# Local transformer kernel: score and weighing matmuls issued in two halves, with a turn of probabilities and a value projection between them

## The chip, the cores and the metric

The kernel runs on one core of one Trainium2 chip. The time is device microseconds of one execution; a kernel is timed several times and the median stands for it. In the rows PE is TensorE (matmuls), PEld its weight loads, DVE is VectorE, ACT ScalarE, POOL GpSimd and SP SyncE.

## The reference

The whole reference has three parts: a time-mixing layer, six layers of a local transformer, and a second block of full attention and a mixture of experts. The change lies in the local transformer, 2048 tokens of width 128 in 2 sequences of 1024:

```python
for i in range(DEPTH):                      # 6 layers
    x = attn_layer(shift_tokens(x), Wqkv[i], q_scale[i], k_scale[i], Wo[i]) + x
    x = ffn_layer(shift_tokens(x), ln_g[i], ln_b[i], W1[i], b1[i], W2[i], b2[i]) + x
...
def attn_layer(x, Wqkv, qs, ksc, Wo):       # 16 heads of 64, windows of 32 tokens
    q, k, v = jnp.split(x @ Wqkv, 3, -1)    # then split into heads
    q, k = l2norm(q) * qs, l2norm(k) * ksc
    # rotary tables on q and k
    out = local_attention(q, k, v)
    return out @ Wo
...
sim = jnp.einsum('bhwie,bhwje->bhwij', bq, bk2) * QK_SCALE   # 32 queries x 64 keys, per window
sim = jnp.where(mask, -jnp.finfo(sim.dtype).max, sim)
attn = jax.nn.softmax(sim, -1)
out = jnp.einsum('bhwij,bhwje->bhwie', attn, bv2)
```

## The kernel before

`time_mixing_and_local` runs the 6 layers as one pipeline over 96 blocks of 128 tokens (`ALL`, 16 blocks in each layer; consecutive blocks belong to the two sequences in turn). A step `i` of the loop over `STEPS` does a different stage for each of several blocks: it turns queries and keys of block i, projects queries and keys of block i+2 and values of block i+1, computes the scores of block i, turns the probabilities of block i-1 and weighs its values, turns the attention of block i-2 and projects it out. The feed-forward works on two blocks together: `variance`, `up` (and `center`) and `down` come in every other step, `up` when i is odd and `down` and `center` when i is even. Each engine has its own program with the same loop, and the order of its work is written out by hand there; the engines meet in semaphores. An engine takes its instructions in order, and so a wait holds all that stands behind it.

A block has 16 heads in 8 pairs (`PAIRS`), and 4 windows (`WPB`). Its scores are 8 x 4 x 2 products of a 64x32 tile of queries with 64 keys; each takes two weight loads and two matmul instructions, so `scores` (L648) is 128 small matmuls and `weigh_v` (L677) another 128. Before the scores, `scores` lays the mask into the two banks with two matmuls (L638, or L641 for a sequence's first blocks). `turn_prob` (L659) turns four pairs of heads at a time with four full-size transposes, and `project_v` (L602 to L604) is three matmuls of 512 columns in a reduced-precision format, high and low parts. `turn_att` is L687, `down` L730, `up` L721 and L722, `center` L707, `variance` L712, `project_out` L699.

The waits that stand ahead of the parts:

- `scores(g)` waits for the turned queries and keys, and for `shifted`, that is until VectorE has read the scores of block g-1.
- `turn_prob(g, 0)` waits for the exponentials of block g.
- `weigh_v(g)` waits for ScalarE's two copies of turned probabilities (`prob_out`, L1018), for the values' DMAs, for `av_out` of the block before, and for VectorE's first shift of block g+1 (`shifted`, L1300), since the scores and the weighed values of neighbouring blocks share three PSUM banks:

```python
SV = (0, 1, 2)
def score_bank(g, par):
    return SV[(4 * g + par) % 3]
def value_bank(g, par):
    return SV[(4 * (g + 1) + 2 + par) % 3]
```

On VectorE `shift_scores(i, 0)` is L1298 (maximum) and L1300 (subtraction), then comes a part of the feed-forward (`norm` L1335 or `finish` L1349), `shift_scores(i, 1)`, `sum_squares(i + 2)` L1271, and `norm_att` L1319. On ScalarE the copies come in the order `empty_prob` (L1018, twice), `empty_v(i + 1, 0)` (L997), `square_qk` (L978), `empty_v(i + 1, 1)`, `exponent(i)` (L1029), and at the end of the step `invert_norms(i + 2)` (L987 to L991).

Of the kernel before, what the change touches and what calls it, by code (L numbers as in the profile page):

```python
# [23 lines left out]
HD = 64  # L24
PAIRS = HEADS // 2
WIN = 32
BLK = 128
WPB = BLK // WIN
# [46 lines left out]
def time_mixing_and_local(nc, A, sb, sem, bank, ident, mean_w, eps, x_main, h_in, h_mid, mod, gate_a):  # L75
# [7 lines left out]
    with ExitStack() as ctx:  # L83
        def buf(name, shape, dt=F32):
            return sb(f"lt_{name}", shape, dt, ctx=ctx)
# [27 lines left out]
        q_t = buf("q_t", [P, 2, PAIRS, BLK])  # L113
        k_t = buf("k_t", [P, 2, PAIRS, WIN + BLK])
        v_tok = buf("v_tok", [P, 2, 2, PAIRS * HD])
        v = buf("v", [P, 2, WPB, PAIRS, HD])
# [4 lines left out]
        prob_t = buf("prob_t", [P, 2, PAIRS, BLK])  # L121
# [19 lines left out]
        S = type("S", (), sems)  # L141
# [26 lines left out]
        def last_flat(t, u):  # L168
            return t[:, 0:CH if u < B + 1 else PAIR]
# [56 lines left out]
        def live(g):  # L226
            return 0 <= g < ALL
# [15 lines left out]
        def has_look(g):  # L243
            return g % SLOTS >= 2
# [49 lines left out]
        def turn_bank(*use):  # L294
            return TURN[uses[use] % len(TURN)]
# [25 lines left out]
# [6 lines that stand above are left out]
        def looks(g):  # L327
            return 32 * ((SLOTS - 2) * (g // SLOTS) + g % SLOTS - 1)
# [4 lines left out]
        with nc.Block(no_gpsimd_drain=True) as blk:  # L333
# [261 lines left out]
            def _(pe):  # L595
# [24 lines left out]
                                          qr[:, g % 2, (4 * j + n) * P:(4 * j + n + 1) * P], ident[:, :])  # L620
                    mm.then_inc(S.turned, 1)

                def scores(g):
                    pe.wait_ge(S.turn_out, 4 * (g + 1))
                    if g == 0:
                        pe.wait_ge(S.cleared, 5)
                        pe.wait_ge(S.cast, 4)
                        pe.wait_ge(T.b_scaled, NCH)

                    if g >= 1:  # L630
                        pe.wait_ge(S.shifted, 2 * g)
                    if g >= 2:
                        pe.wait_ge(S.av_out, 2 * (g - 2) + 1)

                    for par in range(2):
                        f = slice(64 * par, 64 * par + 64)
                        if has_look(g):
                            pe.matmul(bank[:, score_bank(g, par), :], half_b[f, :, :].rearrange("p a k -> p (a k)"), mask[f, :],  # L638
                                      start=True, stop=False, skip_group_check=True)
                        else:  # L640
                            pe.matmul(bank[:, score_bank(g, par), :].rearrange("p (a k) -> p a k", a=PAIRS), ident_b[:, :],  # L641
                                      mask_first[:, :].unsqueeze(1).to_broadcast([P, PAIRS, HD]), start=True, stop=False,
                                      skip_group_check=True)
                    for hp in range(PAIRS):
                        for w in range(WPB):
                            for par in range(2):
                                f = slice(64 * par, 64 * par + 64)
                                mm = pe.matmul(bank[WIN * w:WIN * w + WIN, score_bank(g, par), hp * HD:(hp + 1) * HD],  # L648
                                               q_t[f, g % 2, hp, WIN * w:WIN * w + WIN],
                                               k_t[f, g % 2, hp, WIN * w:WIN * w + 2 * WIN],  # L650
                                               start=False, stop=True, skip_group_check=True)
                    mm.then_inc(S.scores, 1)

                def turn_prob(g, n):
                    if n == 0:
                        pe.wait_ge(S.probs, 2 * (g + 1))
                    wait_free(pe, "prob", g, n)
                    for i in range(4):
                        mm = pe.transpose(bank[:, turn_bank("prob", g, n), i * P:(i + 1) * P],  # L659
                                          prob[:, g % 2, 4 * n + i, :, :].rearrange("p a k -> p (a k)"), ident[:, :])  # L660
                    mm.then_inc(S.prob_turned, 1)

                def weigh_v(g):
                    pe.wait_ge(S.prob_out, 2 * (g + 1))
                    pe.wait_ge(s_v[g % 2], 8 * 16 * (g // 2 + 1))
                    if has_look(g):
                        pe.wait_ge(S.look, looks(g))

                    if g >= 1:
                        pe.wait_ge(S.av_out, 2 * g)  # L670
                    if live(g + 1):
                        pe.wait_ge(S.shifted, 2 * (g + 1) + 1)
                    for hp in range(PAIRS):
                        for w in range(WPB):
                            for par in range(2):
                                f = slice(64 * par, 64 * par + 64)
                                mm = pe.matmul(bank[WIN * w:WIN * w + WIN, value_bank(g, par), hp * HD:(hp + 1) * HD],  # L677
                                               prob_t[f, g % 2, hp, WIN * w:WIN * w + WIN],
                                               v[f, g % 2, w, hp, :], start=True, stop=True)
                    mm.then_inc(S.av, 1)  # L680

                def turn_att(g, n):
                    if n == 0:
# [169 lines left out]
                def last_var(u):  # L853
                    pe.wait_ge(S.last_squared, u + 1)
                    if u >= 1:
                        pe.wait_ge(S.last_scaled, u)
                    pe.matmul(last_flat(bank[:, var_bank(u), :], u), mean_w[:, :], last_flat(last_stat[:, u % 2, :], u),
                              start=True, stop=True).then_inc(S.last_var, 1)
# [36 lines left out]
                for i in STEPS:  # L895
                    if i == -1:
                        group_mean(3)
                        project_output(2)
                        second_mean(2)
                        group_var(3)  # L900
                        second_var(2)
                    if i == 0:
                        project_output(3)
                        second_mean(3)
                    for j in range(4):
                        if live(i):
                            turn_qk(i, j)
                        if live(i + 2):
                            project_qk(i + 2, j)
                        if i == 0 and j == 1:  # L910
                            second_var(3)
                    if even(i, 5) is not None:
                        variance(even(i, 5))
                    if live(i - 2):
                        turn_att(i - 2, 0)
                        turn_att(i - 2, 1)
                    if i == ALL + 1:
                        project_out(ALL - 1)
                        last_mean(0)
                    if live(i):  # L920
                        scores(i)
                    if live(i - 1):
                        turn_prob(i - 1, 0)
                        turn_prob(i - 1, 1)
                    if live(i + 1):
                        project_v(i + 1, 0)
                    if i == ALL + 2:
                        center(CHUNKS - 1)
                    if even(i, 6) is not None:
                        down(even(i, 6))  # L930
                    if i == ALL + 2:
                        last_var(1)
                    if i == ALL + 3:
                        last_mean(2)
                    if i == ALL + 4:
                        last_mean(3)
                        last_var(3)
                    if i == ALL + 5:
                        last_mean(4)
                        last_var(4)  # L940
                    if live(i + 1):
                        project_v(i + 1, 1)
                    if live(i - 1):
                        weigh_v(i - 1)
                    if even(i, 4) is not None and i != ALL + 2:
                        center(even(i, 4))
                    if even(i, 5) is not None:
                        for j in range(FB):
                            up(even(i, 5), j)
                    if i == ALL + 1:  # L950
                        last_var(0)
                        last_mean(1)
                    if i == ALL + 3:
                        last_var(2)
                    if live(i - 2) and i - 2 < ALL - 1:
                        project_out(i - 2)
# [1686 lines left out]
```

## Time and profile before

| | |
|---|---|
| median of 3 runs | 2628.64 us (2627.93 to 2630.3) |
| the profiled execution | 2627.98 us |
| its span, first to last instruction | 2626.1 us |
| mean granted TensorE clock | 0.980 |
| PE busy | 2444.7 us, 93% |
| DVE, ACT, POOL busy | 83%, 77%, 59% |

The local transformer takes the span from about 90 us to about 1640 us. The durations of matmuls are modelled and overlap, so the distances from start to start are what to read; a row of the timeline merges instructions of one line that follow each other, with their count, and in brackets the idle time before the first and what ended it.

### The profile page before, as it was taken

What the parts mean: (1) busy time and instruction counts of PE and PEld (TensorE: products, weight loads), DVE (VectorE), ACT (ScalarE), POOL (GpSimd) and SP (SyncE); (2) the same over time, 40 slices, a digit from 0 to 9 for tenths busy, and PEclk for the clock granted to TensorE, in tenths of its full rate; (3) what the DMA queues carried; (4) which work ended last, traced back from release to release, by engine and by line L of the source; (5) the groups of instructions that cost most, each with busy time, mean ns of one, the idle gap of its engine ahead of it and who ended that gap; (6) DMA issues with size and microseconds to landing.
All of it is one profiled execution on the core that took longest, in us unless ns stands there. A gap on an engine that the chain in (4) does not pass through costs nothing. (4 is left out here: it accounts for less than half of the span.)

```text
span 2626.1 us, 118521 instructions
## 1 busy us (share of the span) xinstructions
PE 2444.7 (93%) x52349; PEld 1964.5 (75%) x52349; DVE 2174.8 (83%) x2455; ACT 2025.0 (77%) x4031; POOL 1536.7 (59%) x1075
## 2 busy tenths in 40 slices
PE   6799999999999999999999999689999999997999
PEld 2478888888787888788888887467777767775787
DVE  5788888888788888888898887388888988885888
ACT  4688888888888888888888887566667666764676
POOL 3788888888788888888897885122323222322111
PEclk8899999999999999999999999899999999999999
DMA  3243434443343344334333333122222222221221
GB/s 99 53 94 92 106 77 94 96 108 83 83 96 97 81 98 100 97 84 95 96 96 78 85 82 76 36 54 52 60 59 61 56 56 59 57 53 34 82 73 41
DMA packets 275793, 202.00 MB, mean 77 GB/s; under 512 B 117569, under 2 KB 215881, under 8 KB 274249
## 3 DMA queue, kind: packets, MB, share of 16 engines
q1 hardware_dynamic: 275280, 194.42, 30.8%
q8 instruction: 414, 6.78, 1.0%
q14 instruction: 99, 0.80, 0.1%
HBM read 36.96 MB, written 1.11 MB: 14 GB/s over the span
## 5 line engine op out<-in xcount | busy, mean ns | idle before, releaser
L509 POOL TENSOR_TENSOR lt_t_sin<-lt_qk,lt_tab 128x512 f32<-128x512 f32 x384 | 684.2, 1802 | 229.2 <-DVE lt_qk L1278 226.7
L514 POOL TENSOR_TENSOR lt_qr<-lt_qr,lt_t_sin 128x1024 f32<-128x1024 f32 x192 | 456.5, 2377 | 28.7 <-POOL lt_t_sin L509 1.8
L2047 DVE TENSOR_REDUCE fa_neg_max<-bank 128x1 f32<-128x1024 f32 x256 | 301.6, 1220 | 94.4 <-PE bank L1855 93.6
L1879 PE MATMUL bank<-fa_prob_t,fa_v 32*64 32x128 f32 x16384 | 279.6, 275 | 29.7 <-issue 25.1
L1969 ACT ACTIVATE fa_prob<-bank,fa_neg_max 128x1024 f32<-128x1024 f32 x128 | 142.7, 1114 | 210.5 <-DVE fa_neg_max L2047 164.3
L2057 DVE STREAM_TRANSPOSE fa_prob_t<-fa_prob 128x1024 f32<-128x1024 f32 x256 | 302.1, 1219 | 0.0
L1879 PEld LDWEIGHTS bank<-fa_prob_t,fa_v 32*64 32x64 f32 x16384 | 241.9, 131 | 77.1 <-issue 55.7
L602 PE MATMUL bank<-lt_w_high,lt_x_high 128*128 128x512 f32 x576 | 280.0, 486 | 0.8 <-ACT lt_v_tok L997 0.4
L1278 DVE TENSOR_TENSOR lt_qk<-lt_qk,lt_rn 128x2048 f32<-128x2048 f32 x96 | 254.5, 2651 | 24.3 <-ACT lt_rn L991 23.0
L619 PE MATMUL bank<-ident,lt_qr 128*128 128x128 f32 x1536 | 233.8, 276 | 13.6 <-POOL lt_qr L514 7.5
L970 ACT COPY lt_qk<-bank 128x512 f32<-128x512 f32 x384 | 229.7, 599 | 16.5 <-POOL lt_t_sin L509 3.8
L1271 DVE TENSOR_REDUCE lt_ssq<-lt_qr 128x32 f32<-128x2048 f32 x96 | 219.0, 2281 | 25.3 <-ACT lt_qr L978 25.3
L619 PEld LDWEIGHTS bank<-ident,lt_qr 128*128 128x128 f32 x1536 | 186.8, 142 | 65.3 <-issue 16.9
L1285 DVE TENSOR_TENSOR lt_qr<-lt_qk,lt_tab 128x2048 f32<-128x2048 f32 x96 | 231.5, 2412 | 3.3
L603 PE MATMUL bank<-lt_w_low,lt_x_high 128*128 128x512 f32 x576 | 228.5, 397 | 0.5 <-issue 0.5
L604 PE MATMUL bank<-lt_w_high,lt_x_low 128*128 128x512 f32 x576 | 228.6, 397 | 0.3 <-issue 0.3
L978 ACT ACTIVATE lt_qr<-lt_qk 128x1024 f32<-128x1024 f32 x192 | 205.5, 1071 | 0.0
L699 PEld LDWEIGHTS bank<-lt_prob_t,lt_w_o 128*128 128x128 f32 x1536 | 187.9, 193 | 8.1 <-issue 1.5
L699 PE MATMUL bank<-lt_prob_t,lt_w_o 128*128 128x128 f32 x1536 | 189.1, 277 | 1.1 <-ACT lt_prob_t L1023 0.8
L1787 POOL TENSOR_TENSOR fa_att_t<-fa_att,fa_inv_all 128x512 f32<-128x512 f32 x32 | 40.7, 1271 | 237.8 <-ACT fa_att L1993 237.8
L677 PEld LDWEIGHTS bank<-lt_v,lt_prob_t 64*32 64x32 f32 x12288 | 129.0, 105 | 67.3 <-issue 65.9
L677 PE MATMUL bank<-lt_v,lt_prob_t 64*32 64x64 f32 x12288 | 149.3, 225 | 27.1 <-issue 25.9
(259 smaller groups left out, 5926.0 us busy)
## 6 DMA issues: line engine op xcount, KB each, us to landing
lt_v<-lt_v_tok SPq DMA_DIRECT2D x576, 128.0 KB, 2.4
fa_v<-fa_v_tok SPq DMA_DIRECT2D x256, 128.0 KB
lt_v<-lt_v_tok SPq DMA_DIRECT2D x192, 64.0 KB, 2.1
lt_k_t<-lt_k_t SPq DMA_DIRECT2D x84, 128.0 KB, 2.6
lt_v<-lt_v SPq DMA_DIRECT2D x168, 64.0 KB, 2.1
lt_w_raw<-in_lt_wqkv_dram SPq DMA_DIRECT2D x36, 256.0 KB, 3.3
ex_cw_all<-cw_kept SPq DMA_DIRECT2D x8, 1024.0 KB, 4.5
lt_x_s<-h_in SPq DMA_DIRECT2D x96, 64.0 KB, 2.7
```

The costliest lines, as they stand in the source:

```text
L509: pool.tensor_tensor(dst[:, :, i, :], src[:, :, 1 - i, :], tab[:, g // 2 % 2, 1, at:at + 32].unsqueeze(1).to_broadcast([P, HEADS, 32]), AL ...
L514: pool.tensor_tensor(qr[:, g % 2, half], qr[:, g % 2, half], t_sin[:, :], ALU.add).then_inc(S.rotated, 1)
L602: pe.matmul(o, xh, w_high[:, k % WS, :], start=True, stop=False)
L619: mm = pe.transpose(bank[:, turn_bank("turn", g, j), n * P:(n + 1) * P], qr[:, g % 2, (4 * j + n) * P:(4 * j + n + 1) * P], ident[:, :])
L677: mm = pe.matmul(bank[WIN * w:WIN * w + WIN, value_bank(g, par), hp * HD:(hp + 1) * HD], prob_t[f, g % 2, hp, WIN * w:WIN * w + WIN], v[f, ...
L699: mm = pe.matmul(o, w_o[:, layer % 2, hp, :], att_t[:, g % 2, hp, :], start=hp == 0, stop=hp == PAIRS - 1)
L970: act.copy(qk[:, g % 2, j * CH:(j + 1) * CH], bank[:, turn_bank("qk", g, j), :]).then_inc(S.proj_out, 1)
L1278: dve.tensor_tensor(heads, heads, r.unsqueeze(2).to_broadcast([P, 2 * HEADS, HD]), ALU.mult)\
L1285: dve.tensor_tensor(qr[:, g % 2, :].rearrange("p (a h d) -> p a h d", a=2, h=HEADS), qk[:, g % 2, :].rearrange("p (a h d) -> p a h d", a=2 ...
L1879: mm = pe.matmul(bank[d, 4 + a, 0:P].rearrange("p (u r) -> p u r", u=UPQ), v[rows, half % 2, kb, d], prob_t[rows, q % 2, par, :, 32 * kb:3 ...
L2047: dve.tensor_reduce(neg_max[:, u % 2, par:par + 1], bank[:, 2 * par:2 * par + 2, :].rearrange("p a n -> p (a n)"), AX.X, ALU.max, negate=T ...
L2057: dve.transpose(prob_t[:, q % 2, par, u % UPQ, :], prob[:, u % 2, par, :]).then_inc(S.turned, 1)
```

## The change

The scores are issued in two halves of four head pairs, and the weighing of values too; the mask and the waits stay ahead of the first half, and the semaphore is raised after the second. Between the halves of the scores stands the first turn of probabilities, between those of the weighing the second projection of values. The first half of the weighing comes after `down` (where there is one) and ahead of `project_v(i + 1, 1)`. The other engines' programs, the order in which the banks of the turns are used, and the number of instructions stay the same.

```diff
--- before.py
+++ after.py
@@ -620,7 +620,22 @@
                                           qr[:, g % 2, (4 * j + n) * P:(4 * j + n + 1) * P], ident[:, :])
                     mm.then_inc(S.turned, 1)
 
-                def scores(g):
+                def scores(g, second):
+
+                    if not second:
+                        lay_mask(g)
+                    for hp in range(4 * second, 4 * second + 4):
+                        for w in range(WPB):
+                            for par in range(2):
+                                f = slice(64 * par, 64 * par + 64)
+                                mm = pe.matmul(bank[WIN * w:WIN * w + WIN, score_bank(g, par), hp * HD:(hp + 1) * HD],
+                                               q_t[f, g % 2, hp, WIN * w:WIN * w + WIN],
+                                               k_t[f, g % 2, hp, WIN * w:WIN * w + 2 * WIN],
+                                               start=False, stop=True, skip_group_check=True)
+                    if second:
+                        mm.then_inc(S.scores, 1)
+
+                def lay_mask(g):
                     pe.wait_ge(S.turn_out, 4 * (g + 1))
                     if g == 0:
                         pe.wait_ge(S.cleared, 5)
@@ -641,15 +656,6 @@
                             pe.matmul(bank[:, score_bank(g, par), :].rearrange("p (a k) -> p a k", a=PAIRS), ident_b[:, :],
                                       mask_first[:, :].unsqueeze(1).to_broadcast([P, PAIRS, HD]), start=True, stop=False,
                                       skip_group_check=True)
-                    for hp in range(PAIRS):
-                        for w in range(WPB):
-                            for par in range(2):
-                                f = slice(64 * par, 64 * par + 64)
-                                mm = pe.matmul(bank[WIN * w:WIN * w + WIN, score_bank(g, par), hp * HD:(hp + 1) * HD],
-                                               q_t[f, g % 2, hp, WIN * w:WIN * w + WIN],
-                                               k_t[f, g % 2, hp, WIN * w:WIN * w + 2 * WIN],
-                                               start=False, stop=True, skip_group_check=True)
-                    mm.then_inc(S.scores, 1)
 
                 def turn_prob(g, n):
                     if n == 0:
@@ -660,24 +666,30 @@
                                           prob[:, g % 2, 4 * n + i, :, :].rearrange("p a k -> p (a k)"), ident[:, :])
                     mm.then_inc(S.prob_turned, 1)
 
-                def weigh_v(g):
-                    pe.wait_ge(S.prob_out, 2 * (g + 1))
-                    pe.wait_ge(s_v[g % 2], 8 * 16 * (g // 2 + 1))
-                    if has_look(g):
-                        pe.wait_ge(S.look, looks(g))
-
-                    if g >= 1:
-                        pe.wait_ge(S.av_out, 2 * g)
-                    if live(g + 1):
-                        pe.wait_ge(S.shifted, 2 * (g + 1) + 1)
-                    for hp in range(PAIRS):
+                def weigh_v(g, second):
+
+                    if not second:
+                        wait_values(g)
+                    for hp in range(4 * second, 4 * second + 4):
                         for w in range(WPB):
                             for par in range(2):
                                 f = slice(64 * par, 64 * par + 64)
                                 mm = pe.matmul(bank[WIN * w:WIN * w + WIN, value_bank(g, par), hp * HD:(hp + 1) * HD],
                                                prob_t[f, g % 2, hp, WIN * w:WIN * w + WIN],
                                                v[f, g % 2, w, hp, :], start=True, stop=True)
-                    mm.then_inc(S.av, 1)
+                    if second:
+                        mm.then_inc(S.av, 1)
+
+                def wait_values(g):
+                    pe.wait_ge(S.prob_out, 2 * (g + 1))
+                    pe.wait_ge(s_v[g % 2], 8 * 16 * (g // 2 + 1))
+                    if has_look(g):
+                        pe.wait_ge(S.look, looks(g))
+
+                    if g >= 1:
+                        pe.wait_ge(S.av_out, 2 * g)
+                    if live(g + 1):
+                        pe.wait_ge(S.shifted, 2 * (g + 1) + 1)
 
                 def turn_att(g, n):
                     if n == 0:
@@ -918,9 +930,12 @@
                         project_out(ALL - 1)
                         last_mean(0)
                     if live(i):
-                        scores(i)
+                        scores(i, 0)
                     if live(i - 1):
                         turn_prob(i - 1, 0)
+                    if live(i):
+                        scores(i, 1)
+                    if live(i - 1):
                         turn_prob(i - 1, 1)
                     if live(i + 1):
                         project_v(i + 1, 0)
@@ -938,10 +953,12 @@
                     if i == ALL + 5:
                         last_mean(4)
                         last_var(4)
+                    if live(i - 1):
+                        weigh_v(i - 1, 0)
                     if live(i + 1):
                         project_v(i + 1, 1)
                     if live(i - 1):
-                        weigh_v(i - 1)
+                        weigh_v(i - 1, 1)
                     if even(i, 4) is not None and i != ALL + 2:
                         center(even(i, 4))
                     if even(i, 5) is not None:
```

## Rows read from the trace of the kernel before

**Rows 1.** The page: busy us, share of the span, instructions; instruction queue: packets, MB.
```profile
PE 2444.7 (93%) x52349; PEld 1964.5 (75%) x52349; DVE 2174.8 (83%) x2455; ACT 2025.0 (77%) x4031; POOL 1536.7 (59%) x1075
...
q8 instruction: 414, 6.78, 1.0%
```

**Rows 2.** Busy time of each engine from 100 to 1600 us.
```profile
100.00:1600.00 1500.00, 1449.00 (x31003) 1222.06 (x31007) 1284.36 (x1338) 1293.20 (x2380) 1241.67 (x736) 0.99 0.39 92
```

**Rows 3.** Waits from 100 to 1600 us: total, times, longest.
```profile
ACT lt_rn L987 <- DVE lt_ssq L1271: 73.6, 49, 1.6
...
PEld bank L677 <- issue: 61.9, 118, 2.2
...
PEld bank L648 <- issue: 33.7, 103, 2.4
...
PE bank L677 <- issue: 23.4, 22, 2.0
...
PE bank L648 <- issue: 9.2, 8, 2.2
```

**Rows 4.** TensorE's timeline in a step with `up`: start, length, instructions.
```profile
922.78 1.48 PE L648 MATMUL bank<-lt_k_t,lt_q_t 64*32 64x64 f32 x128
924.20 1.09 PE L659 MATMUL bank<-ident,lt_prob 128*128 128x128 f32 x8
925.04 0.48 PE L602 MATMUL bank<-lt_w_high,lt_x_high 128*128 128x512 f32 x1
925.37 0.39 PE L603 MATMUL bank<-lt_w_low,lt_x_high 128*128 128x512 f32 x1
...
926.29 0.40 PE L604 MATMUL bank<-lt_w_high,lt_x_low 128*128 128x512 f32 x1
926.62 1.48 PE L677 MATMUL bank<-lt_v,lt_prob_t 64*32 64x64 f32 x128
928.03 0.70 PE L721 MATMUL bank<-lt_f_norm,lt_w 128*128 128x256 f32 x2
```

**Rows 5.** TensorE's timeline in a step with `down`.
```profile
938.54 1.49 PE L648 MATMUL bank<-lt_k_t,lt_q_t 64*32 64x64 f32 x128
...
940.80 0.48 PE L602 MATMUL bank<-lt_w_high,lt_x_high 128*128 128x512 f32 x1
...
941.59 1.46 PE L730 MATMUL bank<-lt_f_gate,lt_w 128*128 128x256 f32 x6
...
945.08 0.70 PE L707 MATMUL bank<-lt_f_x,lt_center_w 128*128 128x256 f32 x2
```

**Rows 6.** Matmuls of L648 begun in two stretches of the step in rows 4.
```profile
922.78:923.39 0.61, 0.60 (x63) 1.00 0.89 334
...
922.78:924.05 1.27, 1.26 (x127) 1.00 0.77 250
```

**Rows 7.** The last turn of attention and the mask ahead of those scores.
```profile
922.26 0.27 PE L687 MATMUL bank<-ident,lt_prob 128*128 128x128 f32 x1
922.47 0.39 PE L638 MATMUL bank<-lt_mask,lt_half_b 64*128 64x512 bf16 x2
```

**Rows 8.** VectorE's timeline in the step of rows 4.
```profile
924.40 0.69 DVE L1298 TENSOR_REDUCE lt_row_max<-bank 128x8 f32<-128x512 f32 x1 [0.85 <-PE bank L648]
925.13 0.69 DVE L1300 TENSOR_TENSOR lt_prob<-bank,lt_row_max 128x512 f32<-128x512 f32 x1
```

**Rows 9.** All engines' timeline where VectorE was late for a weighing.
```profile
597.22 0.69 DVE L1300 TENSOR_TENSOR lt_prob<-bank,lt_row_max 128x512 f32<-128x512 f32 x1
...
598.05 0.28 PE L677 MATMUL bank<-lt_v,lt_prob_t 64*32 64x64 f32 x7
```

**Rows 10.** TensorE's timeline in a weighing with a stall.
```profile
152.77 0.46 PE L677 MATMUL bank<-lt_v,lt_prob_t 64*32 64x64 f32 x32 [1.81 <-issue]
```

**Rows 11.** Timeline of weight loads: idle time at the entry of a small series.
```profile
149.78 1.01 PEld L677 LDWEIGHTS bank<-lt_v,lt_prob_t 64*32 64x32 f32 x97 [0.36 <-issue]
...
922.78 0.30 PEld L648 LDWEIGHTS bank<-lt_k_t,lt_q_t 64*32 64x32 f32 x33 [0.23 <-issue]
```

More of the change, by code:

```diff
@@ L661, in turn_prob @@
                     mm.then_inc(S.prob_turned, 1)
-                def weigh_v(g):
+                def weigh_v(g, second):
+                    if not second:
+                        wait_values(g)
+                    for hp in range(4 * second, 4 * second + 4):
+                        for w in range(WPB):
+                            for par in range(2):
+                                f = slice(64 * par, 64 * par + 64)
+                                mm = pe.matmul(bank[WIN * w:WIN * w + WIN, value_bank(g, par), hp * HD:(hp + 1) * HD],
+                                               prob_t[f, g % 2, hp, WIN * w:WIN * w + WIN],
+                                               v[f, g % 2, w, hp, :], start=True, stop=True)
+                    if second:
+                        mm.then_inc(S.av, 1)
+                def wait_values(g):
                     pe.wait_ge(S.prob_out, 2 * (g + 1))
@@ L672, in weigh_v @@
                         pe.wait_ge(S.shifted, 2 * (g + 1) + 1)
-                    for hp in range(PAIRS):
[L674 to L679, printed above, removed]
-                    mm.then_inc(S.av, 1)
                 def turn_att(g, n):
```

## Prediction

> **What bounds the kernel now.** I read the page first, for its busy shares [rows 1], and then the window that holds 91 or so of the 96 steps of the local transformer [rows 2]. There TensorE has matmuls in flight for 97% of the time; VectorE, ScalarE and GpSimd stand at 86%, 86% and 83%. The granted clock there is 0.99 of full, which is the 2.4 GHz level, so no clock hangs on this change. The page's busy share of TensorE is modelled, so I asked what it waits for [rows 3]: its two largest entries name no other engine but "issue", in front of the two series of small matmuls, L677 (weighing of values) and L648 (scores). TensorE's order is therefore the path, and what matters is how long its instructions take from start to start, plus any wait that a new order brings.
>
> The steps come in two kinds, 48 of each. In one kind `up` follows the weighing (call it an up step), in the other `down` runs between the two value projections (a down step). [Rows 4] is an undisturbed up step: from the first score matmul to what follows the weighing 922.78 to 928.03, 5.25 us. [Rows 5] is an undisturbed down step: 938.54 to 945.08, 6.54 us.
>
> **The change.** No instruction is added or removed. One uninterrupted series of 128 small matmuls (64x32 tiles of the array, eight at a time) becomes two of 64, twice in each step: four turns of probabilities now stand inside the scores, and a value projection inside the weighing. Nothing is moved past a DMA queue. I work out three things: the extra seams, the new distance to VectorE, and what the split gives back of the "issue" stalls.
>
> *A seam, as rows show it.* Leaving a small series: its last matmul starts at 924.05 [rows 6], the first full-size one at 924.20 [rows 4], 0.15 us, where inside the series starts lie 0.01 us apart. Entering one after full 512-column matmuls: 926.29 to 926.62, 0.33, where the four starts from 925.37 to 926.29 are 0.23 apart [rows 4], so 0.10 more. After turns: the last starts at 922.26 and what needs another tile shape at 922.47, 0.21 [rows 7], against 0.11 from turn to turn (eight of them in 0.84 us, [rows 4]), again 0.10. So each split costs some 0.25 us, less what a series gives back that starts afresh: 63 small matmuls start within 0.61 us, 127 within 1.27 [rows 6], so two halves take 1.22. A half is then 0.61 and its exit 0.15, together 0.76. How long a small series takes to hand over to a projection no row shows. The turns hand over to one in 0.03 instead of 0.11 [rows 4], so I bound it by 0.07 and 0.15 and take 0.11; 0.04 us either way is 4 us in all.
>
> *An up step after.* Scores' first half 0.76; four turns 3 x 0.11 and the entry 0.21, 0.54; start of the second half to its last matmul 0.61. From there the other turns (0.15 + 0.33), the hand-over 0.03 and the first projection (0.33 + 0.23 + 0.33) would bring the weighing in 1.40 us. But `weigh_v` waits for the first shift of the new scores, because it writes a bank that VectorE must have read. Before, that was covered by all eight turns and both projections: 2.57 us from 924.05 to 926.62 [rows 4, 6]. VectorE, which had been waiting for the scores, starts its maximum at 924.40 and ends the subtraction at 925.82 [rows 8], 1.77 us after the last score matmul. The release takes 0.14 us more: in one step VectorE was late, its L1300 ended at 597.91 and the weighing began at 598.05 [rows 9]. So the weighing begins 1.91 us after the scores, and TensorE stands still for 0.51 us in each up step. Everything behind it in TensorE's order is held: the projection of values, `up`, the output projection. ScalarE's copies of the turned probabilities must be there too; I put them at nothing, since the first half's copy now starts earlier and the later one is a single copy of 0.6 us after the last turn; were they later than VectorE, the wait would only grow. Then: first half of the weighing 0.61 and hand-over 0.11, projection 0.32 + 0.23 + 0.33, second half 0.76. Sum 0.76 + 0.54 + 0.61 + 1.91 + 0.72 + 0.88 + 0.76 = 6.18, against 5.25: **+0.93 us**.
>
> *A down step after.* Scores and turns 0.76 + 0.54 + 0.76 + 0.36 = 2.42; the first projection 0.79 [rows 5]; six `down` matmuls, whose row is 1.46 long with some 0.38 for the last, so 0.216 from start to start, five of these and an entry of 0.32 (0.216 and the 0.10), 1.40; then 0.72 + 0.88 + 0.76. Sum 6.97 against 6.54: **+0.43 us**. Here `down` covers VectorE (its result is there 1.91 after the scores, the weighing comes after 2.67).
>
> Without stalls this is 48 x (0.93 + 0.43) = **+65 us**. Other engines don't become the bound: ScalarE's copy of the second value projection gets up to 1.1 us later in a down step, but ScalarE then stands idle up to 1.6 us for L1271 anyway (73.6 us over 49 times [rows 3]). I put them at nothing; if that slack were gone, the 1.1 us would cost up to 48 x 1.1 = 53 us.
>
> *What comes back: the instruction stalls.* In one weighing the series stops after 96 of 128 matmuls for 1.81 us with nothing to wait for [rows 10]. The page counts 414 such packets, 6.78 MB, and TensorE's 2 x 52349 instructions are 409 times 256, or 64 bytes each [rows 1]. I read these packets as refills, one per 256 instructions, and the stall as a refill that comes late; they hurt where 256 instructions are used up in about 1.4 us, inside a series. TensorE's matmuls stood so for 23.4 and 9.2 us, 30 times [rows 3]. By the weight loads it is 61.9 + 33.7, of which the usual entry (0.36 and 0.23 in [rows 11], times some 92 each) is 54: 42 us in all. A split spreads such a stretch, but only by what it adds, and that I have already charged: a stall shrinks by the smaller of itself and the added time. 8 stalls in scores at 0.20 are 1.6 us; 22 in the weighing at about 0.5 are 11; the remaining 9 us or so are short ones and go. I take **-20 us** (bounds 0 and -42).
>
> The Trainium skill ("Runtime: NRT & Kernel Launch", Instruction fetch mechanics) has refills in blocks of 256 instructions and calls them mostly hidden. The block size agrees; the 1.81 us of [rows 10] is not hidden.
>
> **The sum.** The profiled execution took 2627.98 us around a span of 2626.1; the median is 2628.64. 2628 + 65 - 20 = **2673 us**, for the median as well, which is 0.6 above.
>
> **Rivals.**
> - *Stalls are not given back.* A refill's own round trip sets the length of a block, and the blocks' borders fall anew. For it: stalls up to 2.0 us long against 0.2 to 0.7 added. Against: a block that is used up more slowly must wait less. 2628 + 65 = 2693.
> - *VectorE is not waited for*, only seams are paid. For it: the 0.51 us rests on one latency added up. Against: VectorE stands idle before the scores, 0.85 us in [rows 8], so its 1.77 can't shrink. 2673 - 48 x 0.51 = 2649.
> - *The other side: seams cost nothing*, as weight loads of the next shape slip under the last tiles. Then no matmul time is added, the turns and the projection only change places, the weighing could begin 2.57 - 0.44 - 0.70 = 1.43 us after the scores (four turns and a projection now stand elsewhere), so the wait for VectorE is 1.91 - 1.43 = 0.48 in up steps (23 us), and all 42 us of stalls can go: 2628 + 23 - 42 = 2609. It decides from the point where a split costs less than about 0.1 us instead of 0.25. For it: weight loads overlap matmuls elsewhere. Against: 0.15, 0.21 and 0.33 of [rows 4, 7] are just such borders.
> - *Another engine falls behind*: ScalarE's later copy delays the exponentials and norms, for the price above in part: 2700 and over.
>
> **How the numbers follow.** My case 0.60 (own range 2657 to 2688), stalls kept 0.12, no wait 0.12, seams free 0.09, another engine 0.07. The range 2642 to 2696 leaves out the seams-free case and most of the last. A measurement of this kernel can tell about 0.2%, 5 us. Faster 0.10: the seams-free case and 0.01 of the no-wait one. Same 0.04: the rest of the no-wait case in which all 42 us of stalls go, 2649 - 22 = 2627. Slower 0.86.
>
> **What would show it.** The steps should be 1.36 us longer in pairs; L677's first half in up steps should begin 1.91 us after the last score matmul, with VectorE's L1300 named as its releaser in some 48 places, about 25 us; L659's turns should come in two groups of four; "issue" waits before small matmuls should fall by some 20 us, while the number of refills stays at 414. Wrong I am if a seam in the new trace is under 0.1 us, if stalls vanish altogether, or if ScalarE or GpSimd shows as releaser of TensorE.

## The result and the profile after

The changed kernel takes 2672.36 us (2668.66 to 2676.22, 4 runs), the kernel before 2629.47 (2627.93 to 2632.09, 4 runs): 1.0155 times as long, 95% interval 1.0135 to 1.0175. That is slower by 43 us; 2673 was forecast. The profiled execution is the fastest of the four, 2668.66 us around a span of 2666.8, 40.7 us more than before.

The page, and the window from 100 to 1600 us, of the kernel after:

```profile
PE 2491.8 (93%) x52349; PEld 1963.6 (74%) x52349; DVE 2154.4 (81%) x2455; ACT 2036.8 (76%) x4031; POOL 1534.4 (58%) x1075
...
q8 instruction: 414, 6.78, 1.1%
...
100.00:1600.00 1500.00, 1452.14 (x30224) 1186.29 (x30223) 1230.07 (x1303) 1272.25 (x2318) 1210.31 (x720) 1.00 0.38 89
```

Against [rows 1, 2] the instructions and the refill packets are the same in number; the same 1500 us hold 30224 matmuls instead of 31003, and all three other engines are less busy. TensorE's order is longer, and nothing else is.

The clock is not quite the same, and the forecast overlooked it ("no clock hangs on this change"). In the kernel before, the granted clock of 0.99 hides seven short stretches at the lower level, 1.2 GHz. Each begins within 0.6 us of the end of a stop in a small series, of 1.97 to 2.43 us from start to start. One of them, in TensorE's timeline of the kernel before and in the window over it (0.50 is the granted clock):

```profile
1054.04 1.47 PE L677 MATMUL bank<-lt_v,lt_prob_t 64*32 64x64 f32 x126
1057.39 0.27 PE L677 MATMUL bank<-lt_v,lt_prob_t 64*32 64x64 f32 x2 [1.88 <-issue]
1057.59 1.04 PE L721 MATMUL bank<-lt_f_norm,lt_w 128*128 128x256 f32 x2
1058.42 1.06 PE L722 MATMUL bank<-lt_f_norm,lt_w 128*128 128x256 f32 x2
...
1058.10:1061.00 2.90, 2.90 (x9) 0.50 0.30 70
```

Two matmuls of `up` take 0.85 us there from start to start, and 0.43 in a usual step. The kernel after has no stop above 1.88 us in its steps, and no stretch at 1.2 GHz.

An undisturbed up step of the kernel after (matmul lines have moved: scores L631, turns L665, weighing L677, `up` L733):

```profile
944.38 0.86 PE L631 MATMUL bank<-lt_k_t,lt_q_t 64*32 64x64 f32 x64
945.17 0.66 PE L665 MATMUL bank<-ident,lt_prob 128*128 128x128 f32 x4
945.76 0.86 PE L631 MATMUL bank<-lt_k_t,lt_q_t 64*32 64x64 f32 x64
946.55 0.66 PE L665 MATMUL bank<-ident,lt_prob 128*128 128x128 f32 x4
946.96 0.48 PE L602 MATMUL bank<-lt_w_high,lt_x_high 128*128 128x512 f32 x1
...
948.32 0.85 PE L677 MATMUL bank<-lt_v,lt_prob_t 64*32 64x64 f32 x64 [0.42 <-DVE lt_prob L1317]
949.10 0.50 PE L602 MATMUL bank<-lt_w_high,lt_x_high 128*128 128x512 f32 x1
...
949.67 0.39 PE L604 MATMUL bank<-lt_w_high,lt_x_low 128*128 128x512 f32 x1
949.99 0.86 PE L677 MATMUL bank<-lt_v,lt_prob_t 64*32 64x64 f32 x64
950.78 0.48 PE L733 MATMUL bank<-lt_f_norm,lt_w 128*128 128x256 f32 x1
```

From the first score matmul to what follows the weighing are 944.38 to 950.78, 6.40 us, where [rows 4] had 5.25. The bracket on the first weighing is the wait that the forecast added up: VectorE's shift (L1317). Beside it VectorE's own timeline:

```profile
946.76 0.69 DVE L1315 TENSOR_REDUCE lt_row_max<-bank 128x8 f32<-128x512 f32 x1 [1.62 <-PE bank L631]
947.48 0.69 DVE L1317 TENSOR_TENSOR lt_prob<-bank,lt_row_max 128x512 f32<-128x512 f32 x1
```

VectorE idles for 1.62 us before the new scores, ends its subtraction at 948.17, and TensorE goes on 0.15 us later. A down step:

```profile
961.10 0.86 PE L631 MATMUL bank<-lt_k_t,lt_q_t 64*32 64x64 f32 x64
961.89 0.66 PE L665 MATMUL bank<-ident,lt_prob 128*128 128x128 f32 x4
...
964.45 1.46 PE L742 MATMUL bank<-lt_f_gate,lt_w 128*128 128x256 f32 x6
965.84 0.86 PE L677 MATMUL bank<-lt_v,lt_prob_t 64*32 64x64 f32 x64
966.62 0.50 PE L602 MATMUL bank<-lt_w_high,lt_x_high 128*128 128x512 f32 x1
...
968.30 0.70 PE L719 MATMUL bank<-lt_f_x,lt_center_w 128*128 128x256 f32 x2
```

7.20 us instead of 6.54 [rows 5], without a wait in it. What TensorE waits for from 100 to 1600 us, after:

```profile
PEld bank L677 <- issue: 67.8, 156, 1.6
...
PEld bank L631 <- issue: 43.3, 185, 1.8
PEld bank L677 <- ACT lt_prob_t L1035: 38.9, 47, 1.0
...
PE bank L677 <- DVE lt_prob L1317: 19.9, 47, 0.6
PE bank L677 <- issue: 17.2, 22, 1.5
...
PEld bank L619 <- issue: 5.0, 8, 3.0
PE bank L631 <- issue: 4.1, 4, 1.7
...
PEld bank L619 <- POOL lt_qr L514: 2.3, 2, 1.5
```

Matmuls of the small series stood at "issue" for 21.3 us, instead of 32.6 [rows 3]. Weight loads show more of it (111 instead of 96), because each step now enters four series instead of two and every entry has a usual gap [rows 11]. And two of the kernel before's waits are nearly gone that the forecast didn't look at (ahead of the turns of queries and keys, L619: at "issue", for GpSimd and for ScalarE):

```profile
PEld bank L619 <- issue: 16.1, 29, 4.0
...
PEld bank L619 <- POOL lt_qr L514: 11.6, 19, 2.9
PE bank L648 <- issue: 9.2, 8, 2.2
PE bank L619 <- ACT lt_q_t L1012: 6.0, 7, 3.8
```

**Adding it up.** I took every distance from one matmul's start to the next, over the 44 up steps and 44 down steps whose matmul order is regular. The median of each distance is a step's usual time, stalls left out; what single steps have above it is the excess.

| us | usual up step | usual down step | excess of 88 steps |
|---|---|---|---|
| before | 15.80 | 15.19 | 59 |
| after | 16.76 | 15.87 | 27 |
| scores split only | 16.08 | 15.47 | 50 |
| weighing split only | 16.12 | 15.52 | 48 |
| `up` in between | 16.30 | 15.85 | 22 |
| scores in quarters | 16.78 | 15.76 | 36 |

A pair of usual steps is 1.64 us longer, 72 us over 44 pairs, and 32 us of excess are gone: 40 together, and the span grew by 40.7. Of the 59 us of excess before, 9.6 are work in six of the stretches at 1.2 GHz; after there are none of these. With the scores split only, and in quarters, it is 5 us each (three stretches), in the other two runs none.

### The profile page after: what moved, and what is told of

It reads as the page before. It is cut to its first block and busy times, and to the rows that moved or that the text cites. A ratio compares the mean times of both kernels' runs of the same rounds, so it can differ in the third digit from the quotient of the medians.

```text
span 2666.8 us, 118521 instructions
## 1 busy us (share of the span) xinstructions
PE 2491.8 (93%) x52349; PEld 1963.6 (74%) x52349; DVE 2154.4 (81%) x2455; ACT 2036.8 (76%) x4031; POOL 1534.4 (58%) x1075
## 5 line engine op out<-in xcount | busy, mean ns | idle before, releaser
L619 PE MATMUL bank<-ident,lt_qr 128*128 128x128 f32 x1536 | 232.3, 275 | 6.9 <-POOL lt_qr L514 4.1
L1295 DVE TENSOR_TENSOR lt_qk<-lt_qk,lt_rn 128x2048 f32<-128x2048 f32 x96 | 231.1, 2407 | 9.2 <-ACT lt_rn L1008 8.5
L619 PEld LDWEIGHTS bank<-ident,lt_qr 128*128 128x128 f32 x1536 | 189.7, 142 | 50.0 <-POOL lt_qr L514 6.3
L677 PEld LDWEIGHTS bank<-lt_v,lt_prob_t 64*32 64x32 f32 x12288 | 137.0, 105 | 116.3 <-issue 73.9
L1315 DVE TENSOR_REDUCE lt_row_max<-bank 128x8 f32<-128x512 f32 x192 | 131.7, 686 | 112.4 <-PE bank L631 112.1
L677 PE MATMUL bank<-lt_v,lt_prob_t 64*32 64x64 f32 x12288 | 170.8, 224 | 42.1 <-DVE lt_prob L1317 22.2
```

The lines of the kernel that those rows point to most:

```text
L619: mm = pe.transpose(bank[:, turn_bank("turn", g, j), n * P:(n + 1) * P], qr[:, g % 2, (4 * j + n) * P:(4 * j + n + 1) * P], ident[:, :])
L1295: dve.tensor_tensor(heads, heads, r.unsqueeze(2).to_broadcast([P, 2 * HEADS, HD]), ALU.mult)\
```

## The experiments

Four kernels ran on one chip, beside a kernel before of 2633.7 us (11 runs). The first two each take half of the change.

**Scores split, weighing whole.**

```diff
-                    if live(i - 1):
-                        weigh_v(i - 1, 0)
                     if live(i + 1):
                         project_v(i + 1, 1)
                     if live(i - 1):
+                        weigh_v(i - 1, 0)
                         weigh_v(i - 1, 1)
```

> The scores in halves with the turn between, the weighing whole and after both value projections as before. My theory (a seam costs TensorE time, VectorE's wait comes only from the early weighing): +0.3 us a step for the seam, 96 x 0.3 = 30 us, no wait for L1317 since 2.1 us lie between the last score matmul and the weighing, some 10 of stalls given back: 2648 us. Rival, seams cost nothing and the whole loss is the wait for VectorE: 2620 to 2629 us.

Measured: 2660.28 us (6 runs), 1.0107 (1.0088 to 1.0126), 27 us over the kernel before. VectorE's shift does not appear among TensorE's waits, as expected. A usual step is 0.28 us longer, up or down alike: that is one seam in the scores, 48 pairs x 0.56 = 27 us. The excess fell by 10 (5 of it the clock's), and the span of the profiled execution grew by 17.9; but that execution (2645.8) was the fastest of the six, and so it and the median don't agree. The median is 12 us above what I expected.

**Weighing split, scores whole.**

```diff
                     if live(i):
                         scores(i, 0)
+                        scores(i, 1)
                     if live(i - 1):
                         turn_prob(i - 1, 0)
-                    if live(i):
-                        scores(i, 1)
-                    if live(i - 1):
                         turn_prob(i - 1, 1)
```

> The weighing in halves around the second value projection, the scores whole with both turns after them. My theory: a seam of 0.37 us in each step, 36 us, and a wait of about 0.2 us in steps with up, 10 us, there for ScalarE's copy of the turned probabilities and not for VectorE, less some 20 of stalls given back: 2655 us, and the gains and losses of the two halves alone add up to about that of the change. Rival, all of the loss is VectorE's wait: no loss here, 2629 or less.

Measured: 2651.82 us, 1.0072 (1.0051 to 1.0092). The wait is there, and it is ScalarE's. Its waits from 100 to 1600 us:

```profile
PEld bank L677 <- ACT lt_prob_t L1033: 25.7, 48, 1.3
...
PE bank L677 <- DVE lt_prob L1315: 1.4, 2, 0.9
```

In a down step, which has no wait, the stretch from the scores to what follows the weighing is 0.35 us longer: the seam in the weighing. In an up step it is 0.51, so the wait for ScalarE's copy costs 0.16 beyond the usual entry. Neither half is worth having alone. VectorE is waited for in numbers only when both halves are there (twice here, 47 times in the change): the split scores end later, and the split weighing begins earlier. By their medians the two halves cost 27 + 18 = 45 us and the change 43, as expected; by the table the pairs are 0.56 + 0.65 = 1.21 us longer against 1.64, and the change gives back more excess (32 against 9 + 11), so the agreement of the sums is in part luck.

**`up` between the halves.** The same four halves, but in up steps both value projections come first and the first of `up`'s four groups stands inside the weighing; seams are as many.

```diff
+                    up_step = even(i, 5) is not None
-                    if live(i - 1):
+                    if live(i - 1) and not up_step:
                         weigh_v(i - 1, 0)
                     if live(i + 1):
                         project_v(i + 1, 1)
+                    if live(i - 1) and up_step:
+                        weigh_v(i - 1, 0)
+                        up(even(i, 5), 0)
...
-                        for j in range(FB):
+                        for j in range(1 if live(i - 1) else 0, FB):
                             up(even(i, 5), j)
```

> As the changed kernel, but in steps with up the second value projection comes ahead of the weighing again, and the first up product stands between its halves: as many seams, the weighing begins 0.7 us later. My theory: the 20 us that TensorE waits for L1317 go, and about as much comes off the time: 2650 us. Rival, that wait only took the place of stalls or of other waits: time as that of the change, 2670.

Measured: 2650.17 us (2642.04 to 2653.77), 1.0066 (1.0048 to 1.0083). The wait for VectorE is down from 19.9 us to 1.9 (4 places), and the usual up step is 0.46 us shorter than the changed kernel's (48 x 0.46 = 22 us; the ratios differ by 0.0089, 23 us). The wait is thus worth what it shows, and little of it is taken back by others. The same edit also takes away the wait of L677's weight loads for ScalarE's copies (38.9 to 3.5 us), so it prices both together.

**Scores in quarters**, two turns between them, weighing whole: `for quarter in range(4): scores(i, quarter); turn_prob(i - 1, quarter)`, each with two pairs of heads and two turns.

> As the run with only the scores split, but in quarters with two turns between: three seams where that has one. My theory: two more seams of 0.25 to 0.3 us each, 96 x 0.55 = 53 us more than that run, a few given back: 2695 us. Rival, a seam is free and the time of the split run comes from where the turns stand: as that run.

Measured: 2683.34 us (5 runs), 1.0199 (1.0179 to 1.0219). The usual pair is 0.99 us longer than with the scores in halves, but the four more seams are only 0.54 of that: from the first score matmul to the first value projection a step takes 2.87 us instead of 2.60, 0.14 for each seam, half of what was expected. The expectation left out that a short series starts faster: a quarter's 32 starts lie within 0.24 us, so two quarters save 0.17 against a half's 0.64. The rest stands in up steps, where 0.35 us more pass ahead of the third group of turns of queries and keys (L619) and 0.10 ahead of the weighing. From 100 to 1600 us:

```profile
PE bank L619 <- ACT lt_q_t L1028: 14.5, 27, 3.8
```

With the scores in halves that wait is 6.5 us, 8 times. In the 88 steps 0.99 x 44 = 44 us less 14 of excess are 30, and with the other steps the two spans are 33 us apart. The medians are 23 apart, since the execution profiled for the halves lay 14 below its median and this one 4. So a seam is not free, and where other engines stand can cost as much as the seams.

**Where the instruction blocks end.** In the kernel before, a usual step issues 679 or 682 of TensorE's instructions (matmuls, weight loads and waits), 1361 in a pair or 5.3 blocks of 256. So the place where a block ends drifts through the series. The trace of before has 36 places inside the small series where more than 0.25 us pass between two starts; counted in instructions modulo 256, all 36 are the same place to within one instruction, and so are all such places in each of the other traces. In 30 of the 36 it lies in the last quarter of the series. I added waits on a semaphore that is long satisfied, some 88 instructions in a step (two waits for one instruction as the profile counts them), among turns and projections, so that the count becomes a multiple of 256 and the end stays where it is put. One list of counts puts it at instruction 110 of 256 in each series of scores (matmul 55), and near matmul 35 of the weighing; the other has 130 fewer at the very start and so ends at 240 (matmul 120) and near matmul 100. Nothing else differs between the two.

```diff
+                def pad(all=False):
+                    n = left[0] if all else -(-left[0] // left[1]) if left[1] > 0 else 0
+                    left[0], left[1] = left[0] - n, left[1] - 1
+                    for _ in range(2 * n):
+                        pe.wait_ge(S.staged, 1)
...
```

> The kernel before with some 88 satisfied semaphore waits added to TensorE's program in each step, spread over the turns, projections and the output projection, so many that a border of 256 instructions falls 110 instructions into every series of scores (and some 70 into every weighing): no block of 256 lies almost wholly inside a series. My theory, stalls are late refills of 256 instructions: TensorE's stops inside L648 and L677 go, some 50 us of them; the added waits take 0.05 us each in TensorE's sequencer, between nothing (hidden under matmuls) and 430 us. Rival, stalls come from DMA traffic or from somewhere else than the place of the border: they stay.

> The same as the run with borders inside, with 130 added instructions fewer in all, so that the border falls 240 instructions into every series of scores and some 200 into every weighing: the block that ends there holds hardly anything but the series. My theory: a stall of 1.5 to 2 us in every series of scores and some in every weighing, 150 to 280 us more than the other run. Rival, the place of the border doesn't matter: the same time as the other run within 10 us.

Measured beside a kernel before of 2635.17: ends inside 2868.09 us, 1.0901 (1.0866 to 1.0937); ends late 3125.38, 1.1883 (1.1841 to 1.1926). 257 us between two kernels that differ in where the blocks end. TensorE's timeline with the ends late:

```profile
1003.35 1.42 PE L662 MATMUL bank<-lt_k_t,lt_q_t 64*32 64x64 f32 x120
1006.58 0.32 PE L662 MATMUL bank<-lt_k_t,lt_q_t 64*32 64x64 f32 x8 [1.81 <-issue]
1006.83 1.09 PE L673 MATMUL bank<-ident,lt_prob 128*128 128x128 f32 x8
...
1010.54 1.19 PE L691 MATMUL bank<-lt_v,lt_prob_t 64*32 64x64 f32 x98
1012.22 0.45 PE L691 MATMUL bank<-lt_v,lt_prob_t 64*32 64x64 f32 x30 [0.49 <-issue]
```

and with the ends inside:

```profile
1002.18 1.48 PE L662 MATMUL bank<-lt_k_t,lt_q_t 64*32 64x64 f32 x128
1003.60 1.09 PE L673 MATMUL bank<-ident,lt_prob 128*128 128x128 f32 x8
...
1007.32 1.48 PE L691 MATMUL bank<-lt_v,lt_prob_t 64*32 64x64 f32 x128
```

The stop comes after exactly the matmul, 120, where the block ends, in 94 of the 96 series of scores. From 100 to 1900 us, late:

```profile
PE bank L662 <- issue: 126.3, 83, 2.1
...
PE bank L691 <- issue: 83.2, 76, 2.0
```

209.5 of the 257 us. From start to start, in the 88 regular steps, the stops are 254 us. Another 34 are the clock's: with the ends late it falls to 1.2 GHz in 22 short stretches of the local transformer, each of them within 2 us of the end of a stop of 1.9 to 2.3 us, with the ends inside in one, at its start; and the rest of a step, where the added waits stand, is shorter with the ends late by some 30 us in all. With the ends inside, L662 has none and L691 one stop of 0.5 us; what is left stands ahead of the projections, where the added waits are:

```profile
PE bank L612 <- issue: 42.3, 169, 0.8
```

The page counts 448 and 447 packets of instructions against 414: 34 and 33 more, for 8740 and 8610 added instructions, again 256 to a packet.

**The change with the ends inside** (same added waits): its cost without stalls in the series.

> The changed kernel with the waits of the run with borders inside. My theory: with stalls out of the way on both sides the change costs its seams and its wait for VectorE alone, which the profile puts at 0.82 us a step: 79 us more than the run of the kernel before with borders inside, where the change itself costs 43. Rival, what the change costs doesn't hang on stalls: 43 us more.

Measured: 2930.19 us, 1.1129 (1.109 to 1.1168), 62 us over the unchanged order with the ends inside. I expected 79, and the rival 43. From the first score matmul to what follows the weighing a pair is 1.82 us longer on average, 87 us in 48, so the seams and the wait are paid in full; the rest of an up step, where the added waits stand, is 0.62 us shorter, 30 us in all (L612's "issue" goes from 42.3 to 29.5). Together 57 of the 62 us. That TensorE gets through added waits while it would stand for VectorE anyway is my reading of this, and not shown by itself.

**The change with the ends late**, on another chip (before: 2629.9, 7 runs), compared by ratios.

> The changed kernel with the waits of the run with late borders, where the kernel before stalls in nearly every series (209 us of TensorE's stops inside L662 and L691, some 1.1 us a series). My theory, a late refill sets the length of a block, and time added inside it is paid out of the stall: the change costs 62 us with borders inside, here well under half of that, 0 to 25 us more than the run with late borders. Rival, seams and stalls add up: 62 to 79 us more.

Measured: 3101.75 us, 1.1804 (1.1785 to 1.1824). It was expected 0 to 25 us above the 1.1883 of the unchanged order, and is 0.0079 or 21 us below it. Its waits from 100 to 1900 us:

```profile
PE bank L691 <- issue: 73.7, 82, 1.6
PE bank L645 <- issue: 71.7, 80, 1.5
```

Stops of 145 us instead of 209.5, 64 less; from start to start, in the 88 regular steps, 66 less (254 to 188). The split adds 1.82 us to a pair, 80 us in 44. That alone would be 14 us more, within what I expected. The other way goes the clock: the 34 us lost at 1.2 GHz are down to 1, since the longest stops are gone. TensorE from 200 to 1800 us, first the unchanged order, then the change, both with the ends late (the granted clock is 0.98 and 1.00):

```profile
200.00:1800.00 1600.00, 1367.64 (x25492) 0.98 0.30 72
...
200.00:1800.00 1600.00, 1407.91 (x25768) 1.00 0.30 72
```

So 80 - 66 - 33 = -19, and the 88 steps are 21 us shorter.

In sum, then, the stops shrink by no more than the time that is added. In a single block they do not follow the seam alone. A stop in the scores goes from 1.74 us to 1.05 on average, 0.69 less (0.58 in up and 0.80 in down steps), where the seam adds 0.30: the block that ends there now also holds the four turns, 0.41 us, and 0.30 + 0.41 = 0.71. The block that ends in the weighing has lost these turns. In up steps seam and wait add 0.84 to it, less 0.41 is 0.43, and the stop is 0.38 shorter; in down steps 0.36 - 0.41 = -0.05, and it is 0.27 longer, which this doesn't explain. So work that is moved is taken from the stop of one block and given to the next; that the whole length of a block is what counts is argued from these rough agreements, not shown.

## Why the prediction was right

*That it gets slower, and by which terms:* shown. The three terms are there, of the expected sign: seams, a wait for VectorE in up steps, and stalls given back. But that the total comes within 2 us is luck: seams and wait cost 22 us more than forecast, and what came back was 21 us more too (12 of excess, most of it the clock's, and 9 in the rest of up steps).

*The seam term, right in kind, too small.* The forecast had 6.18 and 6.97 us; the steps shown take 6.40 and 7.20, so +1.81 a pair instead of +1.36, 87 us instead of 65. A half's last matmul starts 0.643 us after its first, not 0.61: the 63rd start lies where it was counted in [rows 6] plus 0.03. The hand-over to a projection takes 0.15 (bounded by 0.07 and 0.15, taken at 0.11), and four turns with their exit 0.41 instead of 0.36. Each is 0.03 to 0.05, and there are some ten in a pair. The last of these is the first turn after a small series, which takes 0.17 to the second where the forecast had 0.11. [Rows 6] counted matmuls in a longer series; in a series of 64 the first 32 starts lie where they did (0.24), and the last few come later.

*The wait for VectorE:* shown, and of the size forecast. In the step above the weighing begins at 948.32, 1.91 us after the last score matmul (946.41), as forecast; 19.9 us in 47 places, and 22 to 23 us when it is taken away. ScalarE's copies, costed at nothing, do appear as releaser of weight loads of L677 (38.9 us), which the forecast had named as a sign of being wrong. But in each of the 44 regular up steps the second copy ends at least 0.34 us before VectorE's subtraction does, so it adds nothing to the wait; with the scores whole it is what is waited for. It was costed rightly, with 0.34 us to spare.

*What the forecast did not have:* 0.19 us in the rest of a usual up step came back (10.51 to 10.32), 9 us in all, as in the two other runs with the weighing split. Before, it stood ahead of turns of queries and keys (L619, the rows above). That TensorE merely comes later is not the reason: with only the scores split, where it also comes later, the time stays (10.49), and with quarters it grows (10.84). Why it goes with the split weighing is open.

*Stalls given back, -20, and the clock.* 32 us of excess came back. 10 are the clock's, a term that the forecast put at nothing: the kernel before falls to 1.2 GHz after its longest stops, the kernel after has no such stops. (It is one profile of each, and how many long stops an execution has differs.) 11 are stops inside the small series, close to the 1.6 + 11 charged there, and some 11 stand elsewhere, most ahead of turns (L619, L659, L687) and of `up`; without the clock that is 22 against the forecast's 20. "Only by what it adds" holds for the sum; for a single block, what is moved into it or out of it counts too, as the run with the change and late ends shows. That the blocks of 256 instructions set the stalls is shown by the two kernels with 257 us between them, and by the places of the stops in every trace. By the Trainium skill ("Runtime: NRT & Kernel Launch", Instruction fetch mechanics) such refills are mostly hidden; with their ends inside a series they were, with the ends late 209.5 us weren't.

*The rivals.* Stalls not given back: excluded, by "issue" waits and by excess. VectorE not waited for: excluded, by the brackets. Seams that cost nothing: excluded, by +0.28 us a step with the scores alone. Another engine: none falls behind in the change; the busy shares fell and no new ScalarE wait stands outside the weighing (with the scores in quarters the one ahead of L619 grows). A rival that was not named is the clock, and it is worth 10 of the 32 us that came back.

*Left open.* Why the wait ahead of L619 goes with a split weighing and grows with the scores in quarters, and how much of the stalls any one order draws: their number hangs on where ends of blocks fall, and the excess of single profiles spreads with it. No order with these seams was found that beats the kernel before; an order with the ends held inside needs some 88 added instructions in each step, and costs more (233 us) than all the excess here (59).

## What to carry to other kernels

Count the borders between tile shapes on TensorE: the first split of a series costs 0.28 to 0.35 us here, twice a step, before any wait, and a further one 0.14, so a turn put "in the gap" of a series must save more than that. Before moving work out of the shadow between a producer and a consumer, add up the producer's latency (here 1.91 us from the last score to the release) against what still stands in between. Where small instructions come densely, look at stops with no releaser by their place modulo 256 instructions, and remember that an edit may gain or lose there by chance, whatever it was for. And ask for the granted clock of short windows right behind the longest stops: a mean of 0.99 over 1500 us hid 10 us of slow work here.

## What was not expected of the hardware

Where instruction blocks end changed one and the same work by 257 us of 2868: a block of 256 that is used up densely is followed by a stop of up to 2.4 us from start to start. After the longest of these the granted clock fell to 1.2 GHz for a short stretch, 1.6 us of time lost each: after seven of the eight stops above 1.9 us in the kernel before. Waits that are already satisfied aren't free on TensorE: 8740 added instructions of them (two waits each) cost 2868.09 - 2635.17 = 233 us, 0.027 us an instruction, in part hidden and net of the stops that went with them. And the starts inside a series of small matmuls are not even: in the kernel before the 32nd starts at 0.24 us, the 64th at 0.61, the 96th at 0.92 and the 128th at 1.27.
